# The matmul engine's expert program written block by block instead of in a loop, and 39 expert blocks per half instead of 40

## What is computed

```python
T = xt.shape[0]                                   # 8192 tokens
probs = jax.nn.softmax(xt @ Wg, axis=-1)
wts, idx = jax.lax.top_k(probs, K)                # 2 of 8 experts per token
wts = wts / jnp.sum(wts, axis=-1, keepdims=True)
h1 = jax.nn.gelu(jnp.einsum('td,edf->etf', xt, W1) + b1[:, None, :])   # 128 -> 512
ye = jnp.einsum('etf,efd->etd', h1, W2) + b2[:, None, :]               # 512 -> 128
sel = ye[idx, jnp.arange(T)[:, None], :]
moe_out = jnp.sum(wts[..., None] * sel, axis=1).reshape(Bb, Ss, Dd)
return x + moe_out
```

## Time and profile before

| | us |
|---|---|
| median of three runs (1007.47 to 1013.91) | 1008.87 |
| span of the profiled execution | 1007.7 |
| expert stage on the matmul engine | 676 to 917 |
| last gathers, sums and stores, no matmul | 917 to 1007.7 |

### The profile page before, as it was taken

The page is one execution under the profiler, slowest core; times in us unless marked ns, Lnnn a source line. Parts: engine busy times, 40 slices in busy tenths (PEclk is TensorE's granted clock), DMA queues, the critical chain, the costliest instruction groups (busy, mean ns, idle before and its releaser), DMA issues.

```text
span 1007.7 us, 25725 instructions
## 1 busy us (share of the span) xinstructions
PE 768.5 (76%) x8206; PEld 464.6 (46%) x8207; DVE 794.3 (79%) x1681; ACT 635.2 (63%) x1278; POOL 525.7 (52%) x665
## 2 busy tenths in 40 slices
PE   3678776689989898989788888849889999993000
PEld 2445454324445443434344444437777888872000
DVE  7789989788888979898988885168888888888512
ACT  6755468647777777777667778328767777772000
POOL 9600379401254725341133778737886066755775
PEclk9989999869999989999889999559999999997555
DMA  8840015312111111111011120114544355543422
GB/s 196 295 151 1 2 63 182 137 34 59 52 47 55 54 44 55 54 34 34 18 33 57 53 64 26 45 36 122 127 120 130 94 125 130 132 119 111 124 73 73
DMA packets 132214, 84.71 MB, mean 84 GB/s; under 512 B 54534, under 2 KB 117642, under 8 KB 132122
## 3 DMA queue, kind: packets, MB, share of 16 engines
q1 hardware_dynamic: 123930, 66.71, 22.9%
q0 software_dynamic: 8192, 16.79, 6.1%
HBM read 30.77 MB, written 41.94 MB: 72 GB/s over the span
## 4 chain that ended last, share of the span: by engine, by line
PE 59%; issue 9%; ACT 9%; POOL 9%; DVE 9%; DMA 1%; ACTq 0%; DVEq 0%; POOLq 0%; SPq 0%
PE bank L1355 55%; ACT arena L857 5%; POOL HT L758 3%; POOL Z L758 3%; PE bank L1542 2%; PE bank L1359 2%; DVE arena L1044 1%; ACT arena L766 1%; PE bank L1549 1%; POOL xh L496 1%; POOL rr L492 1%; DVE arena L1113 1%; DVE mom L963 1%; DVE Z L1028 1%; ACT arena L933 1%
## 5 line engine op out<-in xcount | busy, mean ns | idle before, releaser
L1113 DVE TENSOR_REDUCE arena<-bank 128x2 f32<-128x512 f32 x512 | 329.7, 686 | 45.3 <-PE bank L1355 41.2
L857 ACT ACTIVATE arena<-bank 128x512 f32<-128x512 f32 x512 | 288.1, 596 | 114.1 <-PE bank L1355 112.1
L1355 PE MATMUL bank<-QK 32*128 32x256 f16 (+1 forms) x2048 | 179.0, 284 | 46.1 <-ACT arena L857 28.2
L1355 PE MATMUL bank<-w2p,QK 128*128 x1280 | 205.0, 246 | 1.9 <-DVE arena L1318 1.9
L1355 PE MATMUL bank<-arena,w1h 128*128 128x256 f16 x640 | 162.5, 277 | 8.5 <-DVE arena L1318 5.0
L685 POOL DMA_INDIRECT expert_in<-HT,idx x128 | 132.4, 1034 | 69.1 <-issue 28.8
L933 ACT ACTIVATE arena<-bank,b1s 128x256 f32<-128x256 f32 x320 | 125.4, 474 | 50.5 <-PE bank L1355 44.8
L1355 PE MATMUL bank<-arena,VA 128*32 128x256 f32 x2048 | 145.5, 404 | 0.7 <-ACT arena L857 0.7
L1355 PEld LDWEIGHTS bank<-w2p,QK 128*128 128x128 f16 x1280 | 123.7, 97 | 13.1 <-issue 2.4
L1355 PEld LDWEIGHTS bank<-QK 32*128 32x128 f16 (+1 forms) x2048 | 51.2, 93 | 169.1 <-ACT arena L857 133.0
L1308 DVE TENSOR_TENSOR QK<-arena,QK 128x1024 f16<-128x1024 f32 x80 | 98.0, 1225 | 19.1 <-ACT QK L766 17.1
(11 more groups left out here) (155 smaller groups left out, 1142.4 us busy)
## 6 DMA issues: line engine op xcount, KB each, us to landing
QK<-qk_parts SPq DMA_DIRECT2D x96, 128.0 KB, 2.6
expert_in<-arena SPq DMA_DIRECT2D x40, 256.0 KB, 3.6
expert_out<-arena SPq DMA_DIRECT2D x80, 128.0 KB
qk_parts<-arena SPq DMA_DIRECT2D x16, 512.0 KB, 3.0
X<-x SPq DMA_DIRECT2D x8, 512.0 KB, 5.8
wst<-w SPq DMA_DIRECT2D x16, 256.0 KB, 2.8
out<-arena SPq DMA_DIRECT2D x16, 256.0 KB, 2.4
expert_in<-HT,idx POOLq DMA_INDIRECT x128
```

The lines of the kernel that those rows point to most:

```text
L857: nc.scalar.activation(PT[t % 8], bank[3 + t % 2][:, :], ACT.Exp, scale=DH ** -0.5)\
L1113: V.tensor_reduce(nmax[n % 2][:, :, 4 * j + g], bank[u % 3][:, :].rearrange("p (q t) -> p q t", q=2), AX.X, ALU.max, negate=True).then_inc ...
L1355: return nc.tensor.matmul(dst, lhsT, rhs, start=start, stop=stop)
```

## The change

The number of blocks per half is no longer rounded up, so `HBLK` = 39 and `NBLK` = 78. `blocks` is adapted to numbers that are no multiple of four: the loops of ScalarE, VectorE and SyncE still start at block 4, are still cut at block 32, now end before block 68, and the last ten blocks are written out. The matmul engine no longer uses `blocks`: its program has all 81 steps one after the other, with constants in the waits, no carried registers, and the wait for the second half's table placed before the first load that needs it. The work per block is the same on every engine.

```diff
-    BLK0.append(BLK0[-1] + -(-(2 * (q1 - q0) * SL // BS + NE - 1) // 4) * 4)
+    BLK0.append(BLK0[-1] + 2 * (q1 - q0) * SL // BS + NE - 1)
...
-            cut = HBLK // 4 - 2
-            for r0, r1 in ((1, cut), (cut, NBLK // 4 - 2)) if second_part else ((1, NBLK // 4 - 2),):
+            cut, end = (HBLK - 7) // 4, NBLK // 4 - 2
+            for r0, r1 in ((1, cut), (cut, end)) if second_part else ((1, end),):
...
-            for b in range(NBLK - 8, NBLK):
+            for b in range(4 * end, NBLK):
                 body(b, b % 4)
...
-                    pool.wait_ge(yb_out[s], 8 * BLK0[part + 1])
+                    pool.wait_ge(yb_out[s], 16 * ((BLK0[part + 1] + 1 - s) // 2))
...
-            carried = [pe.alloc_register(f"expert{k}") for k in range(4)]
-
-            def experts(b, q):
-                looped = not isinstance(b, int)
-                u, qu = b + 3, (q + 3) % 4
-                base = q if looped else b
-                if looped and q == 0:
-                    known.clear()
-                    known.update((k, pe.snap(carried[k], min_val=0, max_val=NE - 1)) for k in range(4))
-                if not looped and b == NBLK - 8:
-                    known.clear()
-                for x, k in ((u, base + 3), (b, base)):
-                    if exists(x) and k not in known:
-                        known[k] = expert_of(x)
+
+            def experts(b):
+                q, u, qu = b % 4, b + 3, (b + 3) % 4
+                for x in (u, b):
+                    if exists(x) and x not in known:
+                        known[x] = expert_of(x)
...
                     if turn == 4 and exists(b + 4):
-                        known[base + 4] = expert_of(b + 4)
-                    if turn == 8 and (looped and q == 3 or not looped and b == 3):
-                        for k in range(4):
-                            pe.reg_mov(carried[k], known[4 + k])
-
-            blocks(pe, -3, experts, second_part=lambda: pe.wait_ge(tab_ready, 2))
+                        if b + 4 == HBLK:
+                            pe.wait_ge(tab_ready, 2)
+                        known[b + 4] = expert_of(b + 4)
+
+            for b in range(-3, NBLK):
+                experts(b)
```

More of the change, by code:

```diff
@@ L1688, in experts @@
                     used(pe, gelu_done, u - 1)
-                    ups = up(u, qu, known[base + 3])
+                    ups = up(u, qu, known[u])
                 if exists(b):
@@ L1692, in experts @@
                     used(pe, yb_ready, b - 1)
-                    downs = down(b, q, known[base])
+                    downs = down(b, q, known.pop(b))
                 for turn in range(12):
```

## The result

The changed kernel takes 996.05 us at the median of 8 runs (993.72 to 1003.18), the kernel before, run beside it, 1008.17 (1004.54 to 1013.91). The ratio is 0.9866, with a 95% interval of 0.9833 to 0.9899: faster by 10 to 17 us. The forecast was 994.0, in a range of 984 to 1003.

What follows compares the result with a forecast made beforehand. The matmul engine bounds the kernel, followed by a 90.32 us gather tail. Two blocks fewer 5.3, plain iterations 5.9, additions 0.6 and the loop's end 3.1 sum to 14.9: 1008.87 - 14.9 = 994.0 us, range 984 to 1003.

Steps and rivals of the forecast that it cites:

- I had taken the duration for a constant: TensorE's load of the expert's number in written-out steps: it costs 0.02 us with a lead and 0.52 without.

Runs made afterwards that it cites:

- e9_adds_after_scatters: The changed kernel with GpSimd's four additions cut into quarters and put behind the last scatter; 990.19 us, ratio 0.9850 to the kernel before.

## What to carry to other kernels

When a step's excess is a scalar load on an engine's own sequencer, write down for some forty steps when the load ends after the head and how long the step is: an exact line tells the price, and moving the load is one edit that tests it. Here moving the load within the loop took more off the stage (8.3 us) than writing out the whole loop (6.1). Before a faster stage is trusted, look at each wait that stands in a queue ahead of stores, and note by how much it passes.

## What the runs showed of the hardware

- A register load (TENSOR_LOAD) on TensorE's sequencer takes 0.30 us, but up to 0.58 if it starts 0.80 to 1.00 us behind the start of a store's issue on SyncE: in blocks 28 to 67 all 11 such loads of before last 0.36 us or more and 24 of 27 in after, while the other 29 of before stay under 0.33. With stores and transposing loads issued later the median fell from 445 to 302 ns. I had taken the duration for a constant; that the store is the cause is not shown by a run.
- The sequencer's lead decides by a sharp edge: up to 0.71 us after the step's head the load is free, and beyond it every 0.01 us of the load is 0.01 us of the step, in 40 steps of 40 of after.
- GpSimd's quarter additions of 128x256 take 0.72 us in some places and 1.71 in others beside VectorE (`e9_adds_after_scatters`); this was not followed up.
